# The opening of the value stage: the contexts of batches 0 and 1 first, then x of batches 0 and 1

## What is computed

```python
n = layernorm(x)                        # over the 512 features
h = concatenate([ctx, n], axis=1)       # 256 keys per batch
q, k, v = n @ Wq, h @ Wk, h @ Wv        # 4096, 512, 512 columns
x = x + softmax(q k^T / sqrt(128)) v @ Wo
f = layernorm(x)
r = softmax(f @ gate_w.T)
out = x + ((f * (r @ in_scale)) @ sign(weight).T) * (r @ out_scale) + bias
```

## Time and profile before

| | us |
|---|---|
| median of 3 runs | 683.64 (683.36 to 684.81) |
| the profiled execution | 685.01 |
| its span, first to last instruction | 683.2 |
| TensorE matmuls busy in it | 670.4 (98%) |
| DVE busy | 437.2 (64%) |
| ACT busy | 356.9 (52%) |
| GpSimd busy | 301.7 (44%) |

### The profile page before, as it was taken

How to read it: one execution, slowest core, us unless ns; L and a number is a source line. 1 busy time by engine, 2 the same in 40 slices (tenths; PEclk the granted TensorE clock), 3 DMA queues, 4 the chain that set the end, 5 groups by cost and what they waited for, 6 DMA issues and landing times.

```text
span 683.2 us, 10608 instructions
## 1 busy us (share of the span) xinstructions
PE 670.4 (98%) x3376; PEld 564.8 (83%) x3376; DVE 437.2 (64%) x817; ACT 356.9 (52%) x882; POOL 301.7 (44%) x249
## 2 busy tenths in 40 slices
PE   6999999999999999999999999999999999999997
PEld 4888888888888888888888888888888888878875
DVE  4562232766666666666666666666666666667866
ACT  3334232755565556545655565556555644566553
POOL 4235000552374337324632463246334638754586
PEclk9999999999999999999999999999999999998999
DMA  9566695556557876655587766565887555544502
GB/s 330 206 220 220 242 371 219 178 191 210 189 179 261 273 255 210 216 188 198 198 280 248 253 189 222 187 201 194 270 276 250 195 203 193 184 159 129 184 33 78
DMA packets 83671, 144.86 MB, mean 212 GB/s; under 512 B 8040, under 2 KB 41064, under 8 KB 82592
## 3 DMA queue, kind: packets, MB, share of 16 engines
q1 hardware_dynamic: 83616, 144.19, 61.6%
HBM read 91.60 MB, written 52.56 MB: 211 GB/s over the span
## 4 chain that ended last, share of the span: by engine, by line
PE 95%; DVE 2%; ACT 1%; DMA 1%; issue 1%; SPq 0%; ACTq 0%; DVEq 0%
PE bank L1146 52%; PE bank L1265 25%; PE bank L1250 13%; PE bank L1343 2%; DMA raw_a<-in_L_xattn_Wv 1%; PE bank L1292 1%; PE bank L1300 1%; PE bank L1155 1%; PE bank L1315 0%; PE bank L1163 0%; DVE stats L838 0%; DVE bank L950 0%; DVE oT L835 0%; ACT oT L565 0%; PE bank L1357 0%
## 5 line engine op out<-in xcount | busy, mean ns | idle before, releaser
L477 POOL TENSOR_TENSOR p_low<-p_low,p_high 128x1024 fp32r<-128x1024 f32 x64 | 153.7, 2402 | 269.0 <-ACT p_high L565 269.0
L1265 PE MATMUL bank<-wo_pair,oT 128*128 128x512 f32 x768 | 190.4, 395 | 1.2 <-DVE oT L835 1.1
L1146 PE MATMUL bank<-xT,wq_pair 128*128 128x512 f32 x768 | 184.9, 390 | 0.0
L1265 PEld LDWEIGHTS bank<-wo_pair,oT 128*128 128x128 f32 x768 | 141.2, 190 | 28.6 <-issue 1.9
L1146 PEld LDWEIGHTS bank<-xT,wq_pair 128*128 128x128 f32 x768 | 140.1, 188 | 25.9
L654 ACT ACTIVATE prob<-bank,nmax 128x256 f32<-128x256 f32 x256 | 119.1, 471 | 49.6 <-DVE nmax L919 44.4
L936 DVE STREAM_TRANSPOSE p_turned<-prob 128x512 f32<-128x512 f32 x128 | 91.1, 712 | 63.4 <-ACT prob L654 63.4
L565 ACT ACTIVATE oT<-bank 128x512 fp32r<-128x512 f32 x64 | 38.3, 598 | 165.5 <-DVE bank L950 165.5
L919 DVE TENSOR_REDUCE nmax<-bank 128x2 f32<-128x512 f32 x128 | 88.0, 690 | 52.4 <-PE bank L1146 51.8
L1146 PEld LDWEIGHTS bank<-kg,qT 128*128 128x128 f32 x768 | 108.4, 191 | 9.8 <-issue 0.2
L1146 PE MATMUL bank<-kg,qT 128*128 128x256 f32 x768 | 111.8, 283 | 0.0
(11 more groups left out here) (96 smaller groups left out, 614.4 us busy)
## 6 DMA issues: line engine op xcount, KB each, us to landing
p_park<-p_turned SPq DMA_DIRECT2D x64, 512.0 KB, 2.6
p_low<-p_park SPq DMA_DIRECT2D x64, 512.0 KB, 5.3
r_all<-r_park SPq DMA_DIRECT2D x64, 256.0 KB, 4.0
v_park<-v_stage SPq DMA_DIRECT2D x8, 1024.0 KB, 4.3
raw_a<-in_L_xattn_Wq SPq DMA_DIRECT2D x32, 256.0 KB, 4.6
raw_b<-in_L_xattn_Wo SPq DMA_DIRECT2D x32, 256.0 KB, 4.6
k_park<-k_stage SPq DMA_DIRECT2D x8, 1024.0 KB, 4.9
kg<-k_park SPq DMA_DIRECT2D x32, 256.0 KB, 4.8
```

The costliest lines, as they stand in the source:

```text
L477: nc.gpsimd.tensor_tensor(part, part.bitcast(fp32), p_high[:, :].rearrange("p i c q -> p (i c q)"), ALU.subtract).then_inc(p_lo, 1)
L1146: last = nc.tensor.matmul(dst, left(a, c), right(b, c), start=(n == 0), stop=(n == 3 * chunks - 1))
L1265: last = nc.tensor.matmul(wo_bank[:, :], oT[:, s, h, :], wo_pair[:, w, h, :], start=((s, w) == TERMS[0] and h == 0), stop=((s, w) == TERMS ...
```

## The change

The value stage gets a list of units, `v_units`, in the order (batch, kind) = (0, context), (1, context), (0, x), (1, x), and from batch 2 on as before. All engines walk through that list. In detail:

- SyncE: the four chunks of Wv follow context 0 directly, then context 1, x 0, x 1; before, x 0 stood between the second and third chunk. The store of a batch waits until the later of its two units is done: three units for batch 0 (two before), four for batch 1 as before.
- TensorE: the transposes of context 1 stand inside product 0, in front of its third term; those of x 0 inside product 1, in front of its third term; those of x 1 behind product 1. Product 1 waits for the whole low part of its operand (before: for the high part first, the low part ahead of the second term).
- ACT: the high part of context 1 right after the fourth high part of Wv; then for each unit the high part of the operand two places ahead in the list, then that of the product.
- DVE: the statistics of batch 0 between the second and third low part of Wv, the low part of context 1 after the fourth, then the norm of batch 0 and the statistics of batch 1; for unit 0 the low part of x 0, the norm of batch 1, the statistics of batch 2, and then the low part of product 0.

```diff
--- before.py
+++ after.py
@@ -206,6 +206,11 @@
 
         half_ready, half_scaled, half_out = sem("half_ready"), sem("half_scaled"), sem("half_out")
 
+
+
+        v_units = [(0, 0), (1, 0), (0, 1), (1, 1)] + [(b, kc) for b in range(2, B) for kc in range(KC)]
+        position = {unit: n for n, unit in enumerate(v_units)}
+
         block = es.enter_context(nc.Block())
 
         def count(g, per_quad, qd, k):
@@ -272,10 +277,11 @@
 
             load_c(0)
             for c in range(HC):
-                if c == 2:
-                    load_x(0)
                 sp.dma_start(raw_a[:, c, :], wv[c * P:(c + 1) * P, :]).then_inc(wv_in[c], 16)
-            for b in range(1, B):
+            load_c(1)
+            load_x(0)
+            load_x(1)
+            for b in range(2, B):
                 load_c(b)
                 load_x(b)
                 if b == 4:
@@ -285,7 +291,7 @@
             sp.dma_start(bias_b[:, :], ffn_b.rearrange("(a n) -> a n", a=1).broadcast_to((P, D))
                          ).then_inc(bias_in, 16)
             for b in range(B):
-                sp.wait_ge(proj_lo, 2 * b + 2)
+                sp.wait_ge(proj_lo, max(position[b, kc] for kc in range(KC)) + 1)
                 sp.dma_start(v_park[:, :, b].rearrange("g p s c k -> p g (s c k)"),
                              words(v_stage[:, b % 2]).rearrange("p g s c k -> p g (s c k)")
                              ).then_inc(v_parked[b % 2], 16)
@@ -584,19 +590,17 @@
                 split_hi(wv_pair, raw_a, c, wv_hi)
                 if c == 0:
                     ct_half(0)
-            xt_half(0)
-            for b in range(B):
-                if b >= 2:
+            ct_half(1)
+            for n, (b, kc) in enumerate(v_units):
+                if kc == 0 and b >= 2:
                     act.wait_ge(v_parked[b % 2], 16 * (b // 2))
-                for kc in range(KC):
-                    n = 2 * b + kc
-                    if b + 1 < B:
-                        (ct_half, xt_half)[kc](b + 1)
-                    act.wait_ge(proj_ready, n + 1)
-                    copy(v_stage[:, b % 2, :, HI, kc, :],
-                         proj_bank[n % 2][:, :].rearrange("p (g d) -> p g d", g=G)
-                         ).then_inc(proj_hi, 1)
-                if b == 5:
+                if n + 2 < len(v_units):
+                    nb, nkc = v_units[n + 2]
+                    (ct_half, xt_half)[nkc](nb)
+                act.wait_ge(proj_ready, n + 1)
+                copy(v_stage[:, b % 2, :, HI, kc, :],
+                     proj_bank[n % 2][:, :].rearrange("p (g d) -> p g d", g=G)).then_inc(proj_hi, 1)
+                if (b, kc) == (5, 1):
                     act.wait_ge(wk_in, 16)
                     for c in range(HC):
                         split_hi(wk_pair, raw_b, c, wk_hi)
@@ -858,33 +862,35 @@
                          part[:, HI]).then_inc(ct_lo, 1)
 
             ct_rest(0)
-            dve.wait_ge(x_in[0], 16)
-            layer_stats(0, 0)
             for c in range(HC):
                 dve.wait_ge(wv_hi, c + 1)
                 subtract(wv_pair[:, LO, c, :], raw_a[:, c, :], wv_pair[:, HI, c, :]
                          ).then_inc(wv_lo, 1)
+                if c == 1:
+                    dve.wait_ge(x_in[0], 16)
+                    layer_stats(0, 0)
+            ct_rest(1)
             layer_norm(0, 0)
             dve.wait_ge(x_in[1], 16)
             layer_stats(1, 1)
-            xt_rest(0)
-            layer_norm(1, 1)
-            for b in range(B):
-                for kc in range(KC):
-                    n = 2 * b + kc
-                    if b + 1 < B:
-                        (ct_rest, xt_rest)[kc](b + 1)
-                    if b + 2 < B:
-                        if kc == 0:
-                            dve.wait_ge(x_in[b + 2], 16)
-                            layer_stats(b + 2, b + 2)
-                        else:
-                            dve.wait_ge(xt_ready, b + 1)
-                            layer_norm(b + 2, b + 2)
-                    dve.wait_ge(proj_hi, n + 1)
-                    subtract(v_stage[:, b % 2, :, LO, kc, :],
-                             proj_bank[n % 2][:, :].rearrange("p (g d) -> p g d", g=G),
-                             v_stage[:, b % 2, :, HI, kc, :]).then_inc(proj_lo, 1)
+            for n, (b, kc) in enumerate(v_units):
+                if n + 2 < len(v_units):
+                    nb, nkc = v_units[n + 2]
+                    (ct_rest, xt_rest)[nkc](nb)
+                if n == 0:
+                    layer_norm(1, 1)
+                row = n // 2 + 2
+                if row < B:
+                    if n % 2 == 0:
+                        dve.wait_ge(x_in[row], 16)
+                        layer_stats(row, row)
+                    else:
+                        dve.wait_ge(xt_ready, row - 1)
+                        layer_norm(row, row)
+                dve.wait_ge(proj_hi, n + 1)
+                subtract(v_stage[:, b % 2, :, LO, kc, :],
+                         proj_bank[n % 2][:, :].rearrange("p (g d) -> p g d", g=G),
+                         v_stage[:, b % 2, :, HI, kc, :]).then_inc(proj_lo, 1)
             for u in range(G * NHALF):
                 if u == 6:
 
@@ -1166,27 +1172,24 @@
 
             pe.wait_ge(const_ready, 2)
             ct_transpose(0)
-            for b in range(B):
-
-                for kc, (src, lo_sem) in enumerate(((cT, ct_lo), (xT, xt_lo))):
-                    n = 2 * b + kc
-                    if n < 2:
-                        pe.wait_ge((ct_hi, xt_hi)[n], 1)
-                    else:
-                        pe.wait_ge(lo_sem, b + 1)
-                    if n >= 2:
-                        pe.wait_ge(proj_lo, n - 1)
-                    product(proj_bank[n % 2][:, :],
-                            lambda s, c: src[:, s, c, b * T:(b + 1) * T],
-                            lambda s, c: wv_pair[:, s, c, :], HC,
-                            (wv_hi, wv_lo) if n == 0 else None,
-                            {0: {1: lambda: pe.wait_ge(ct_lo, 1)},
-                             1: {1: lambda: pe.wait_ge(xt_lo, 1)}}.get(n, {})
-                            ).then_inc(proj_ready, 1)
-                    if n == 0:
-                        xt_transpose(0)
-                    if b + 1 < B:
-                        (ct_transpose, xt_transpose)[kc](b + 1)
+            for n, (b, kc) in enumerate(v_units):
+                src, lo_sem = ((cT, ct_lo), (xT, xt_lo))[kc]
+                if n == 0:
+                    pe.wait_ge(ct_hi, 1)
+                else:
+                    pe.wait_ge(lo_sem, b + 1)
+                if n >= 2:
+                    pe.wait_ge(proj_lo, n - 1)
+                product(proj_bank[n % 2][:, :],
+                        lambda s, c: src[:, s, c, b * T:(b + 1) * T],
+                        lambda s, c: wv_pair[:, s, c, :], HC,
+                        (wv_hi, wv_lo) if n == 0 else None,
+                        {0: {1: lambda: pe.wait_ge(ct_lo, 1), 2: lambda: ct_transpose(1)},
+                         1: {2: lambda: xt_transpose(0)}}.get(n, {})
+                        ).then_inc(proj_ready, 1)
+                if 0 < n < len(v_units) - 2:
+                    nb, nkc = v_units[n + 2]
+                    (ct_transpose, xt_transpose)[nkc](nb)
 
             pe.wait_ge(gate_in, 16)
             pe.wait_ge(xt_lo, B)
```

## The result

The changed kernel takes 685.90 us (median of 5 runs, 685.34 to 687.12) against 683.64 us (median of 5, 683.04 to 685.32) for the kernel before: ratio 1.0032, 95% interval 1.0020 to 1.0044. In a later series beside 23 runs of the kernel before it was 1.0045 (1.0030 to 1.0059; 6 runs, median 686.82 against 683.74). The forecast was 685.7.

What follows compares the result with a forecast made beforehand. TensorE was taken to bound the kernel, so product 2's later start (+1.75 us) and the late store of batch 0 (+0.34) carry through: 683.64 plus 2.09 gives 685.7 us, 0.31% more; range 684.2 to 688.0.

Steps and rivals of the forecast that it cites:

- Bound and carry-over: TensorE alone sets the pace from 16.50 to 132.00 us, so any shift of product 2's start carries on whole.
- Part 1: Opening loads: last two Wv pieces land 0.67 us earlier, x of batch 0 2.0 us later, at 8.33 us.
- Part 2: Product 0 and context 1: transposes at 9.98 us, product 1 at about 12.46, 0.61 us earlier; Wv's low parts hidden.
- Part 3: Product 2 waits for DVE to empty product 0's bank behind other work, starting at 18.22 instead of 16.47: +1.75 us.
- GpSimd's chain: Batch 0's statistics to 1/sigma take 4.05 us; batch 1's 1/sigma comes at 15.77, 0.48 us before DVE wants it.
- rival 1: Opening chains are shorter and batch 0's store lands in time: 0 to 1.3 us slower, say 684.5; chance 0.22.
- my floor for product 2: Batch 1's norm must wait for its 1/sigma, so product 2 cannot start before 17.78 us, or +1.31.
- Part 4: Batch 0's store, released a unit later, lands in 4.2 us, 0.48 late for ACT; product 6 0.34 us later.
- The second: Something larger: store lands in 6.4 us (total 687.9) or TensorE's clock falls behind opening gaps (688.0); chance 0.12.
- The third (faster): TensorE's own order decides the opening, product 0's bank emptied by 14.8: gain of 1.7 us, 681.9; chance 0.04.
- The sum: Whole kernel: 1.75 for product 2's start plus 0.34 for the store's wait, 2.09 on median 683.64: 685.7 us.

Runs made afterwards that it cites:

- e6: Changed kernel, banks of products 0 and 1 emptied first, x 0 transposes one term earlier, x 1's inside product 2, store wait at the write: 683.26 us, ratio 0.9994.
- e7: Kernel before with the new order of loads alone: product 2 at 19.59 us, profiled span 686.3 us.
- e12: Kernel before, unedited, profiled a second time: 684.26 us, product 2 at 17.84 us.
- e8: Changed kernel, unedited, profiled again: 684.36 us (its series 686.82), product 2 at 17.40 us.
- e5: Changed kernel with product 0's bank emptied first and ACT's store wait directly ahead of the write: 684.35 us, ratio 1.0012.
- e10: Changed kernel, unedited, profiled again: 690.34 us, product 2 at 18.60 us.
- e9: Changed kernel, unedited, profiled again: 684.74 us, product 2 at 17.84 us.
- e11: Changed kernel, unedited, profiled again: 685.29 us, product 2 at 18.39 us.
- e4: Kernel before, only batch 0's store waits for the third unit instead of the second: product 2 to 6 13.27 us instead of 12.88, span 681.5 us.
- e2: Changed kernel, ACT's store wait moved directly ahead of the value buffer's first write: product 2 to 6 12.89 us instead of 13.33, span 685.7 us.
- e3: Changed kernel with the old order of loads: 686.27 us, ratio 1.0038, product 2 at 20.03 us.

## Why the prediction was right

By its own steps, the first profile of the changed kernel beside what was said:

- **Bound and carry-over.** Right: from product 6 to the end both kernels take 651.8 us, where the clock holds.
- **Part 1, the loads.** x of batch 0 at 8.44 (said: 8.37; 7.96 to 8.69 in the other profiles of the changed kernel). There the rule that the place in the stream sets the landing held within 0.4 us; with the same order of loads e6 and e7 are 0.7 to 0.8 us off (9.06 and 9.10 instead of 8.33). Wv's last piece landed between 6.47 and 8.78 us over all profiles, and the 17.84 of product 2 in e12 goes with the 8.78.
- **Part 2.** Transposes of context 1 at 10.09 (9.98), ACT's copy at 11.18 (11.11), DVE's low part at 11.81 (11.74). The low parts of Wv were hidden as said.
- **Part 3.** Right in mechanism, +2.26 us in place of +1.75 in the first pair of profiles. The transposes of x 0 stood at 14.78 instead of 14.38. Half of that is product 1 at 12.65 instead of 12.46; the other half its eight matmuls, 2.13 us instead of 1.92: I had the clock rise in product 0, as before, but it rose at 13.17, behind the start of product 1. For the same reason there was no gap in front of product 1, where I had 0.7 us. The rest, 0.11 us, is the step from DVE's end to TensorE's start: 18.59 to 18.73 is 0.14 us, where I took 0.03. From DVE's 16.05 to 17.93 are 1.88 us, as summed (0.60 + 0.46 + 0.82). In the other profiles the same sum starts from 14.71 to 15.92 and gives 17.40 to 18.60: a mean of 18.2 over the five.
- **GpSimd's chain** was mis-sized the other way: from batch 0's statistics to its 1/sigma 3.52 us (8.44 to 11.77 + 0.19), not 4.05. The third of its five steps took 0.34 us where it had taken 0.88; in the kernel before it ran while DVE subtracted the low parts of Wv, here these were over. So at least this 0.54 us was no cost of the first use, which rival 1 thought the whole 1.2 us might be. The chain was not on the path, but its length made my floor for product 2 too high by about half a us, as e8 shows with 17.40.
- **Part 4.** +0.45 us (13.33 against 12.88), said +0.34; the difference is again the step of 0.14 us, taken as 0.03. The store landed in 4.2 us, as taken.
- **Rivals.** The first (nearly nothing) did not come: even e5, with the bank of product 0 and the store off the path, has 1.0012. The second was real and perhaps had too little chance: one profile in five. Whether it is why the second series stood at +3.1 us no profile shows. It also shows that the tail was read too lightly: I took the full pace behind a gap of 0.71 us as evidence against a fall, and overlooked that the very profile I read has one from 615.2 us on. The rule of the Trainium skill that I cited there, page TensorE: Matmul & The Clock Gate, section "HAM oscillation — how this bites in real kernels", that waits between bursts can put the array back to half its clock, is told there of waits longer than any gap here, so it did not make this rival likelier as I wrote. That gaps of under 1 us can be enough is shown by e7 (0.85 us) and e10 (0.95 and 0.83 us); in e8, e9 and e11 gaps of the sizes of e10's did nothing. The third (faster) needed DVE's order changed; e6 does that, among other things, and its median is 0.5 us under the kernel before, within its interval.
- **The sum.** The medians differ by 2.26 us, 2.09 said. Part of that agreement is luck. The 16.47 that the sum starts from is an early start: the second profile of the kernel before has 17.84. The pair of profiles has 2.7 us at product 6, but in the four profiles of the changed kernel without a fall in the opening product 6 is at 31.4 on average, in the two of the kernel before at 30.0, 1.4 us apart. A fairer measure is the time from the landing of Wv's last piece to product 2: 8.8 to 9.1 us in the old order of units (the two profiles and e4), 10.9 to 11.8 in the new (the five, e2 and e3). By the means that is 2.3 us more; less the 0.67 by which the piece comes earlier in the stream it is 1.7, near the 1.75 said for part 3. What made the medians what they are is not settled. Of fourteen timed executions of the changed kernel four had a mean clock of 1.00 and took 684.36 to 685.34 us; ten had less and took 685.89 to 690.34. But a lower mean clock need not be the cost: in the first profile (0.998) the fall cost 0.3 us and the late start the rest. The falls, which cost from nothing to 3.1 us (e10) in an execution, were not in the sum.

## What to carry to other kernels

When the order of units changes on the bounding engine, write down for each other engine what now stands ahead of the step that frees a buffer: here a finished product lay 5 us in its bank because two queues took work for a later unit first. A wait belongs directly ahead of the instruction that needs it; moved up by one instruction it cost 0.4 us. And compare kernels by the starts of a few landmarks and the time between them, in several profiles of each, not by two spans.

## What the runs showed of the hardware

TensorE's granted clock fell to half behind gaps that were each short: 0.95 and 0.83 us within 2.4 us (e10), 1.90 us (e10 again), 0.85 us (e7), 1.22 us (before, at 615 us). Gaps of about the same sizes left it at full in other executions (0.93 and 0.83 us in e8, likewise e9 and e11; 1.20 and 1.00 us in e12, near 614 and 618 us). The falls lasted 3 to 7 us. The two in e10 cost 1.6 and 1.5 us, the one in the first profile of the kernel before 2.1, the one at 617 us in the changed kernel's profile 0.3 (652.04 against 651.8). The Trainium skill, page TensorE: Matmul & The Clock Gate, section "Seeing it yourself", warns that the clock's records are not always reliable; here the durations agree with them, 4.59 against 3.03 us for twelve matmuls. In the opening the column says 1.00 while matmuls start 0.43 us apart, but there the trace has no clock record at all: the first begins at 11.06 us in the kernel before and at 13.17 in the changed kernel, just where the distance between matmuls goes from 0.43 to 0.24 us.

GpSimd's small steps of 1/sigma were slower while DVE subtracted the low parts of Wv. The third step of batch 0's chain took 0.85 to 0.88 us in the four profiles where it met these subtractions (before, e12, e4, e7) and 0.34 to 0.35 in the ten where they were over. The second step always met them in batch 0's chain and took 0.86 to 0.87 us; for batch 1 it took 0.56. No edit tested this; it is the same in all fourteen profiles. The third step in the first profile of the kernel before, then in that of the changed kernel:

```profile
8.98 0.88 POOL L443 TENSOR_SCALAR nwt<-rstd,vare 128x1 f32<-128x1 f32 x1
```

```profile
11.07 0.34 POOL L449 TENSOR_SCALAR nwt<-rstd,vare 128x1 f32<-128x1 f32 x1
```

A store of 1024 KB landed in 4.1 to 4.6 us in 67 of 112 cases. Those of batches 3 and 7 took 5.1 to 5.2 us in every profile, batch 1's 5.5 to 6.4 in ten of fourteen, and batch 0's 4.2 in thirteen and 5.9 in e10; why is open.
